# Attentions of successive images side by side, with banks of their own, in a network of four layers

## The reference: what is computed

```
# layer 0: attention with 32 channels           x = Wp @ softmax(q k / sqrt(32)) v + x
# layer 1: bottleneck with a deformable 3x3 convolution
off = conv3x3(h); y, x = grid + off             # per pixel and tap: where to sample
samp = bilinear(h, y, x) * sigmoid(mask)        # 9 taps x 4 corners, gathered
x = relu(bn(w3 @ relu(bn(w2 @ samp))) + x)
# layer 2: attention with 16 query channels     x = gamma * (softmax(q k) v) + x
# layer 3: group norm, then attention with 128 channels
h = group_norm(x); w = softmax(q(h) k(h) / sqrt(128))
x = (x + Wp @ (w v(h))) / sqrt(2)
```

## Time and profile before

| | |
|---|---|
| device time, median of 3 runs | 571.77 us (570.62 to 573.72) |
| profiled execution, its own time | 573.63 us |
| its span, first to last instruction | 571.6 us |
| busy: PE, DVE, ACT, POOL | 491.7, 316.8, 288.4, 293.3 us |
| mean granted TensorE clock | 0.91 of full |

### The profile page before, as it was taken

One profiled execution on the slowest core, in us unless ns is written; L12 is line 12 of the kernel. 1 busy time (PEld: TensorE's weight loads), 2 busy tenths in 40 slices (PEclk: granted clock), 3 DMA queues, 4 the chain that ended last, 5 costly groups with the idle time before them and its releaser, 6 DMA issues.

```text
span 571.6 us, 7362 instructions
## 1 busy us (share of the span) xinstructions
PE 491.7 (86%) x2688; PEld 328.6 (57%) x2688; DVE 316.8 (55%) x558; ACT 288.4 (50%) x485; POOL 293.3 (51%) x292
## 2 busy tenths in 40 slices
PE   5897897869889778889998969998957999896996
PEld 3443633525435346856686845776844677693775
DVE  4746225476556766766678556558565525624321
ACT  4275461374177655245575434584532557442652
POOL 0000177777777777777777777777777300000000
PEclk9999778659879879979999979999987899997999
DMA  5000111112212111211313111112111100100000
GB/s 218 0 1 1 46 56 50 56 47 58 86 46 94 46 52 48 55 47 46 94 47 92 52 46 52 50 54 87 52 52 46 28 1 1 38 1 0 1 1 37
DMA packets 12562, 26.92 MB, mean 47 GB/s; under 512 B 4976, under 2 KB 5616, under 8 KB 12528
## 3 DMA queue, kind: packets, MB, share of 16 engines
q0 software_dynamic: 9216, 18.89, 11.7%
q1 hardware_dynamic: 2880, 6.52, 3.0%
q10 hardware_dynamic: 432, 1.05, 0.5%
HBM read 21.99 MB, written 4.46 MB: 46 GB/s over the span
## 4 chain that ended last, share of the span: by engine, by line
POOL 49%; PE 26%; issue 15%; DVE 3%; ACT 3%; DMA 2%; POOLq 0%; DVEq 0%; ACTq 0%
POOL got L298 49%; PE pd L604 5%; PE pq L596 2%; PE pc L586 2%; PE pa L586 2%; PE pq L363 2%; PE pa L334 2%; DMA xall<-x_dram 1%; PE pa L541 1%; PE pc L541 1%; DVE neg_max L1601 1%; PE pc L388 1%; PE pc L334 1%; PE pa L570 1%; PE pd L328 1%
## 5 line engine op out<-in xcount | busy, mean ns | idle before, releaser
L298 POOL DMA_INDIRECT got<-cell_table,rows_all x288 | 293.1, 1018 | 155.4 <-issue 87.5
L1601 DVE TENSOR_REDUCE neg_max<-pa 128x1 f32<-128x1024 f32 x48 | 58.7, 1223 | 39.7 <-PE pa L334 39.3
L604 PEld LDWEIGHTS pd<-v3T,probsT 128*128 128x128 f32 x512 | 60.3, 192 | 11.1 <-ACT probsT L1112 8.5
L604 PE MATMUL pd<-v3T,probsT 128*128 128x128 f32 x512 | 63.3, 277 | 3.2 <-ACT probsT L1112 2.4
L363 PE MATMUL pq<-q_stack,k_stack 128*128 128x512 f32 x120 | 55.1, 516 | 9.5 <-ACT expT L1141 5.1
L334 PE MATMUL pa<-k_stack,q_stack 96*128 96x512 f32 x96 | 40.2, 505 | 10.5 <-DVE neg_max L1601 7.3
L1141 ACT ACTIVATE expT<-pq 128x512 f32<-128x512 f32 x64 | 35.6, 595 | 23.9 <-PE pq L363 23.0
L363 PEld LDWEIGHTS pq<-q_stack,k_stack 128*128 128x128 f32 x120 | 24.6, 217 | 36.2 <-ACT expT L1141 11.9
L1678 DVE TENSOR_TENSOR weighed<-got,corner_w 128x1152 f32<-128x1152 f32 x32 | 43.3, 1354 | 3.2 <-DMA got<-cell_table,rows_all 2.1
L1112 ACT ACTIVATE probsT<-pq 128x1024 f32<-128x1024 f32 x32 | 32.7, 1022 | 15.0 <-PE pq L596 10.3
L1225 ACT ACTIVATE expT<-pq 128x512 f32<-128x512 f32 x56 | 31.1, 598 | 15.4 <-PE pq L363 14.3
(11 more groups left out here) (173 smaller groups left out, 788.6 us busy)
## 6 DMA issues: line engine op xcount, KB each, us to landing
got<-cell_table,rows_all POOLq DMA_INDIRECT x288, 2.5
cell_table<-tabS SPq DMA_DIRECT2D x4, 512.0 KB, 2.6
out_dram<-cells SPq DMA_DIRECT2D x8, 256.0 KB, 2.1
xall<-x_dram SPq DMA_DIRECT2D x2, 512.0 KB, 8.6
wts<-weights_dram SPq DMA_DIRECT2D x1, 778.5 KB, 6.1
xall<-x_dram ACTq DMA_DIRECT2D x2, 256.0 KB, 5.2
xall<-x_dram ACTq DMA_DIRECT2D x1, 512.0 KB, 8.4
cell_table<-tabS SPq DMA_DIRECT2D x4, 64.0 KB, 2.7
```

The source lines that it names most:

```text
L298: nc.gpsimd.indirect_dma_start(got[:, t, k, :], None, tables[b % 2], bass.IndirectOffsetOnAxis(ap=rows_all[:, b, at:at + 1], axis=0)).then ...
L604: last = nc.tensor.matmul(d0[:, 0:C], probsT[:, tile(j)], v3T[:, j, :], start=j == 0, stop=j == TILES - 1)
L1601: nc.vector.tensor_reduce(neg_max[:, t:t + 1], pair[:, :], axis=X, op=ALU.max, negate=True)\
```

## The change

1. Banks. For images 1 and 2, layer 3 has pa for its scores, b0 for turned probabilities, v and end, and d0 for values. Layer 2 has pc for qk, scores and (as c0, c1) values, and b1 for v and shifted scores. Layer 2 of the last image alternates shifted scores between b1 and d1. Layer 3 of the last image, which has no partner, alternates between pairs again, and its turned halves between b0 and b1.
2. Halves. l3_turn(b, t) becomes l3_turn(b, t, g): 4 transposes and one ACT copy of 512 columns for each half g. l2_v and l3_v work by halves in one bank.
3. Order. All lists of calls are new. l3(b) and l2(b + 1) are woven together from their first tiles to their last, for b = 0, 1, 2. Layer 3 of image b therefore starts when layer 1 of image b + 1 is about to end. The lists of layers 0 and 1 are new as well, and the very first calls too: l0_v(0) stands ahead of l0_qk(0, 0).

Number and shape of the matmuls stay as they are; there are 32 more ACT copies for the turned halves (64 of 512 columns for 32 of 1024), and 4 more for l2_v.

```diff
-
-        def e2_bank(h, j):
-            return (b0, b1)[j % 2] if h == 0 else (b0, b1, a0)[j % 3]
-
-        def e_free(h, j):
-
+
+
+        LAST = BATCH - 1
+
+        def w3_banks(b):
+            return pc if b else pa
+
+        def v2_bank(b, h):
+            return b1 if b else (c0, c1)[h]
+
+        def s2_pair(b):
+            return pc if b else pa
+
+        def shift2_bank(b, h):
+            if b == 0:
+                return (b1, c1)[h]
+            return c1 if b == LAST and h else d1
+
+        def e2_bank(b, h, j):
+            if b == 0:
+                return (b0, b1)[j % 2] if h == 0 else (b0, b1, a0)[j % 3]
+            return (b1, d1)[j % 2] if b == LAST else b1
+
+        def e_free(b, h, j):
+
+            if b:
+                return max(TILES * h + j - (b == LAST), 0)
             return {(0, 0): 0, (0, 1): 0, (1, 0): TILES - 1, (1, 1): TILES, (1, 2): 0}.get(
                 (h, j), TILES * h + j + 1 - (2, 3)[h])
 
-        def o2_bank(t):
-            return (a1, c0, d0)[t % 3][:, 0:C + 1]
+        def o2_bank(b, t):
+            return ((c0, c1)[t % 2] if b else (a1, c0, d0)[t % 3])[:, 0:C + 1]
+
+        def tr2_bank(b, h):
+            return (b1, c0)[h] if b else (c1, b0)[h]
+
+        def k3_banks(b):
+            return pc if b == LAST else pa
+
+        def v3_bank(b, h):
+            return (b0, b1)[h] if b == LAST else b0
+
+        def s3_pair(b, t):
+            return (pa, pc)[t % 2] if b == LAST else pa
+
+        def pt_bank(b, g):
+            return (b0, b1)[g] if b == LAST else b0
+
+        def o3_bank(b, t):
+            return ((d0, d1)[t % 2] if b == LAST else d0)[:, 0:C]
+
+        def tr3_bank(b, h):
+            return (b0, b1)[h] if b == LAST else b0
 
         @block.sync
         def _(sp):
...
                 if b == 0:
                     pe.wait_ge(shift0_done, 2 * BATCH)
                 else:
-                    pe.wait_ge(exp3_done, TILES * b - 1)
+                    pe.wait_ge(mom_ready, b)
                 for c in (0, 2, 1, 3):
                     if c == 1:
                         pe.wait_ge(w3_mm, 4 * b + 2)
-                    nc.tensor.matmul(pa[:, c * N // 4:(c + 1) * N // 4], wt("w3")[quarter(c), :], h2[quarter(c), :],
+                    nc.tensor.matmul(w3_banks(b)[:, c * N // 4:(c + 1) * N // 4], wt("w3")[quarter(c), :], h2[quarter(c), :],
...
-                if b == 0 and t:
-                    pe.wait_ge(max2_done, t)
-                if b and t == 1:
-                    pe.wait_ge(v2_ready, b + 1)
-                if b and t >= 2:
-                    pe.wait_ge(max2_done, TILES * b + t - 1)
-                scores(t, 0, s2_pair(b, t), s2_mm)
+                else:
+                    pe.wait_ge(max2_done, TILES * b + t)
+                scores(t, 0, s2_pair(b), s2_mm)
 
...
             def l2_shifted(b, h, j):
                 if j == 0:
                     pe.wait_ge(shift2_done, 2 * b + h + 1)
-                if e_free(h, j):
-                    pe.wait_ge(exp2_done, 2 * TILES * b + e_free(h, j))
-                shifted_scores(h, j, 0, e2_bank(h, j), t2_mm)
+                    pe.wait_ge(v2_ready, 2 * b + 2)
+                if e_free(b, h, j):
+                    pe.wait_ge(exp2_done, 2 * TILES * b + e_free(b, h, j))
+                shifted_scores(h, j, 0, e2_bank(b, h, j), t2_mm)
...
             def l3_k(b, h):
                 pe.wait_ge(h3_ready, 2 * b + h + 1)
-                nc.tensor.matmul(pc[:, half(h)], wt("wk3"), h3[:, half(h)], start=True, stop=True).then_inc(k3_mm, 1)
+                if b and b < LAST:
+                    pe.wait_ge(exp3_done, TILES * b)
+                nc.tensor.matmul(k3_banks(b)[:, half(h)], wt("wk3"), h3[:, half(h)], start=True, stop=True).then_inc(k3_mm, 1)
 
             def l3_q(b, h):
                 pe.wait_ge(h3_ready, 2 * b + h + 1)
+                if b < LAST:
+                    pe.wait_ge(k3_ready, 2 * b + h + 1)
+                else:
+                    pe.wait_ge(exp3_done, TILES * b)
                 nc.tensor.matmul(pa[:, half(h)], wt("wq3"), h3[:, half(h)], start=True, stop=True).then_inc(q3_mm, 1)
...
             def l3_scores(b, t):
                 if t == 0:
                     pe.wait_ge(q3_ready, 2 * b + 2)
                     pe.wait_ge(k3_ready, 2 * b + 2)
-                if t >= 2:
+                elif b < LAST:
+                    pe.wait_ge(exp3_done, TILES * b + t)
+                elif t >= 2:
                     pe.wait_ge(exp3_done, TILES * b + t - 1)
-                pair = (pa, pc)[t % 2]
                 for h in range(2):
-                    last = nc.tensor.matmul(pair[:, half(h)], q3[:, tile(t)], k3[:, half(h)], start=True, stop=True)
+                    last = nc.tensor.matmul(s3_pair(b, t)[:, half(h)], q3[:, tile(t)], k3[:, half(h)], start=True, stop=True)
                 last.then_inc(s3_mm, 1)
 
-            def l3_turn(b, t):
+            def l3_turn(b, t, g):
+
                 pe.wait_ge(exp3_done, TILES * b + t + 1)
+                copies = 2 * (TILES * b + t) + g - (b == LAST)
                 if t == 0:
                     pe.wait_ge(v3_ready, 2 * b + 2)
-                else:
-                    pe.wait_ge(pt_copied, TILES * b + t)
+                if t or (g and b < LAST):
+                    pe.wait_ge(pt_copied, copies)
+                for j in range(4):
+                    last = nc.tensor.transpose(pt_bank(b, g)[:, tile(j)], probs[:, t % 2, tile(4 * g + j)], ident)
+                last.then_inc(pt_mm, 1)
+
+            def l3_values(b, t):
+                pe.wait_ge(pt_copied, 2 * (TILES * b + t) + 2)
+                if b < LAST and t:
+                    pe.wait_ge(o3_norm, TILES * b + t)
+                elif b == LAST:
+                    if t >= 2:
+                        pe.wait_ge(o3_norm, TILES * b + t - 1)
+                    elif t:
+                        pe.wait_ge(exp2_done, 2 * TILES * BATCH)
                 for j in range(TILES):
-                    last = nc.tensor.transpose(pq[:, tile(j)], probs[:, t % 2, tile(j)], ident)
-                last.then_inc(pt_mm, 1)
-
-            def l3_values(b, t):
-                pe.wait_ge(pt_copied, TILES * b + t + 1)
-                if t:
-                    pe.wait_ge(o3_norm, TILES * b + t)
-                for j in range(TILES):
-                    last = nc.tensor.matmul(d0[:, 0:C], probsT[:, tile(j)], v3T[:, j, :], start=j == 0, stop=j == TILES - 1)
+                    last = nc.tensor.matmul(o3_bank(b, t), probsT[:, tile(j)], v3T[:, j, :], start=j == 0, stop=j == TILES - 1)
                 last.then_inc(o3_mm, 1)
...
-            def l3_turn(b, t):
-                act.wait_ge(pt_mm, TILES * b + t + 1)
-                if t:
+            def l3_turn(b, t, g):
+                act.wait_ge(pt_mm, 2 * (TILES * b + t) + g + 1)
+                if t and g == 0:
                     act.wait_ge(o3_mm, TILES * b + t)
-                copy(probsT[:, :], pq[:, :]).then_inc(pt_copied, 1)
+                copy(probsT[:, half(g)], pt_bank(b, g)).then_inc(pt_copied, 1)
...
```

More of the change, by code:

```diff
@@ L766, in _ @@
             l0_out(2, 3)
             l0_turn(2, 3)
-            for n in range(6):
+            l1_conv1(2, 0)
+            l0_scores(3, 5)
+            l0_scores(3, 6)
+            l1_conv1(2, 1)
+            l0_scores(3, 7)
+            l0_shift(3, 0)
+            l0_shift(3, 1)
+            l0_shifted(3, 0, 0)
+            l0_shifted(3, 0, 1)
+            l1_table(2, 0)
+            l1_turn(0, 5)
+            for n in range(2, 5):
                 l0_shifted(3, 0, n)
-            l1_turn(0, 3)
@@ L853, in _ @@
[L853 to L855 removed]
+            l1_turn(1, 4)
+            l1_turn(1, 5)
             l3_k(0, 0)
@@ new lines, in _ @@
+            l2_scores(2, 4)
+            l3_turn(1, 2, 0)
+            l2_shifted(2, 0, 0)
+            l3_scores(1, 4)
+            l2_shifted(2, 0, 1)
+            l3_turn(1, 2, 1)
+            l2_scores(2, 5)
+            l2_shifted(2, 0, 2)
+            l2_shifted(2, 0, 3)
+            l2_scores(2, 6)
+            l3_values(1, 2)
+            l3_turn(1, 3, 0)
+            l3_scores(1, 5)
+            l3_turn(1, 3, 1)
+            l2_shifted(2, 0, 4)
+            l2_scores(2, 7)
+            l1_turn(3, 1)
@@ new lines, in _ @@
+            for n in range(5, 8):
+                l2_shifted(2, 0, n)
+            l2_shift(2, 1)
+            l3_values(1, 3)
+            l3_turn(1, 4, 0)
+            l2_shifted(2, 1, 0)
+            l2_values(2, 0)
+            l3_turn(1, 4, 1)
+            l2_shifted(2, 1, 1)
+            l2_shifted(2, 1, 2)
+            l2_values(2, 1)
+            l1_turn(3, 2)
+            l2_shifted(2, 1, 3)
+            l3_values(1, 4)
+            l2_shifted(2, 1, 4)
+            l3_scores(1, 6)
+            l2_shifted(2, 1, 5)
@@ L972, in _ @@
+            l3_turn(1, 7, 0)
+            l2_turn(2, 1)
+            l3_turn(1, 7, 1)
+            l1_turn(3, 5)
+            l3_end(1, 0)
+            l3_groups(2)
```

(11 more changed lines are left out.)

1524 lines of the change are left out of this document (814 added, 710 removed).

## The result

| | median us | of runs | profiled run, its span, clock |
|---|---|---|---|
| before | 572.05 | 570.62 to 573.72 (4) | 573.63, 571.6, 0.910 |
| changed | 580.28 | 579.42 to 580.91 (4) | 579.42, 577.4, 0.905 |

The ratio is 1.0137 with a 95% interval of 1.0106 to 1.0168, so the changed kernel is 8 us slower. The profiled execution is its fastest; the spans of the other three are 577.9 to 578.9. Ratios in this text leave out two executions that ran far above the others of their kernel (one of old_front at 1019 us, one of the new order at five taps at 579.7).

What follows compares the result with a forecast made beforehand. Time was taken as the last gather's landing plus PE's remaining work: 450.0 + 2.9 + 71.2 + 6.4 + 46.5 = 577.0 us of span, 5.4 above 571.6, so a median of 577.2 us, range 569.5 to 584.5.

Steps and rivals of the forecast that it cites:

- Last landing at 450.0: End of GpSimd's gathers: first gather 1 us earlier at 67.4, train length kept, last data landing at 450.
- the head's loss: Image 0's start: l0_v(0) ahead of l0_qk(0) makes the cells 1.5 to 2 us later.
- The turn of the last tile at 452.9, 2.9 us behind it: Tile (3, 7): weighing, adding and PE's turn take 2.9 us after landing, so the turn comes at 452.9.
- 14.8 us more behind the turn, less 3.2: PE from l1_turn(3, 7) to l2_turn(3, 1): 14.8 us of l3(2) added, 3.2 taken off, 59.6 becoming 71.2.
- Gain and loss of the weaving: Behind the last turn: filling waits with a second attention and having one pair each were taken to cancel.
- The stalls of "about 5 us": PE from the last turn to l2_turn(3, 1): stalls of about 5 of 59.6 us, left as they were.
- Group norm 6.4: Last image's group norm: 5.7 us plus DVE's l3_end(2, 0) at 0.65, giving 6.4.
- last layer 46.5: Last fourth layer: 50.8 us less 2.8 for q and k at full clock and 1.5 for halves, 46.5.
- Everything ahead costs nothing: All work ahead of image 2's group norm is covered by the gathers, 95.2 us per image, PE needing 86.0.
- Interlocking pairs: Rival: single banks in images 1 and 2 expose waits between engines, 583 to 588 us; chance 0.15 for 581 to 588.
- Weaving pays: Rival: 5 us of stalls behind the turn vanish and the start wins 3, 570 us; chance 0.14 shared with no effect.
- No effect: Rival: PE's whole work sets the time, so order doesn't matter, 571 to 574 us; chance 0.14 shared with weaving.

Runs made afterwards that it cites:

- old_front: Changed kernel with the call lists of the kernel before on PE, ACT and DVE up to image 0's group norm: 579.41 us, ratio 1.0132.
- five taps: 5 of 9 gathers per tile of images 1 to 3: kernel before 566.16 us, changed kernel 571.67, changed kernel with the earlier lists up to image 0's group norm 563.02.
- new front: Changed kernel's call lists up to image 0's group norm; put into the kernel before, all else its own: 587.02 us, ratio 1.0264.
- new rest: Changed kernel's calls behind image 0's group norm; with the kernel before's lists ahead of them ratio 1.0132, with its own 1.0137.
- late_weigh: Changed kernel with weighing and adding of tiles (3, 5) and (3, 6) moved behind l3_norm(2) on DVE, their turns and copies likewise: 583.06 us, ratio 1.0240.
- early_weigh: Kernel before with only l1_weigh and l1_add of (3, 4) and l1_weigh of (3, 5) put between l2_values(2, 1) and (2, 2) on DVE: 583.46 us, ratio 1.0227.
- eight taps: 8 instead of 9 gathers for each tile of image 3: kernel before 567.87 us (ratio 0.9927), changed kernel 573.75 us (1.0019).
- late_weigh_l3: late_weigh, and part of image 2's fourth attention (scores, v, half turns, values) moved ahead of l1_turn(3, 7): 597.26 us, ratio 1.0458.
- old_front_late: late_weigh_l3 with the call lists of the kernel before up to image 0's group norm: 593.61 us, ratio 1.0413.
- new_last: Kernel before with only the last fourth attention as in the changed kernel (call order, halves, values in two banks): 570.79 us, ratio 0.9985.
- old rest: Kernel before's calls behind image 0's group norm; with the changed kernel's lists ahead of them 587.02 us, ratio 1.0264.

## Why the prediction was right

It said 577.2 us for 580.28, and 577.0 for the span of 577.4. The mechanism held: the last tile is turned at nearly the same time as before, and PE has 7.6 us more behind it. One path to that turn I had not seen, and that it meets the one I named is luck.

**Last landing at 450.0.** It was near 450.4, for partly wrong reasons. I had the first gather at 67.4; it was at 69.1, since the rows come at 68.6, 3.6 later than before. The train was 0.8 shorter than I had it (378.8 for 379.6), which gave half of the 1.7 us back. In the other profiles with the new front the rows came at 69.5 to 70.3, with the old one at 64.2 to 66.0. I had put the head's loss at 1.5 to 2 us. Both halves of q and k now wait behind the 16 matmuls of l0_v(0) (the first half ran at 4.97 and is now at 10.93, the first scores at 17.43 for 15.66), which makes 1.8 us. The other 1.9 come further down the list; which calls make them was not tried.

**The turn of the last tile at 452.9, 2.9 us behind it.** It was 453.8. I said that PE would wait and that DVE would be at (3, 6) or (3, 7) when it did. It was at (3, 5): as DVE goes in order, the group norm of image 2 comes 20 us behind that tile's landing, and the turn 7.6 us behind the group norm. These 7.6 us are the same in all five profiles with the new rest as it is, also in the three with fewer gathers, where DVE never waits for data. So in the changed kernel the turn hangs on tile (3, 5) over the group norm, and the last landing, which I had named, comes 0.5 us ahead of its weighing. That both paths end so close is luck, but it also makes the sum robust: in late_weigh, which frees the group norm of tile (3, 5), DVE waits for the last landing (1.9 us), the turn is 2.8 us behind that weighing's start, and nothing is won. (With the gathers of the changed kernel that turn would be at some 453.3, an estimate from 450.4 and 2.8.) So the wait at (3, 5) is not what costs in the changed kernel, and what is left is the l3(2) work behind the turn, which the prediction took from the lists. early_weigh shows what the placing does where that work stands ahead of the turn: with an unchanged list on PE it costs 13 us (10.3 of it at the turn in the profile).

**14.8 us more behind the turn, less 3.2.** 11.6 was forecast. The stretch that the sum has, from the turn to the end of l2_turn(3, 1), took 69.8 us for 71.2 and was 59.6 before. PE is busy in it for 67.5 us where it was for 57.3, so 10.2 longer, and idle for 2.3 us both times. Gain and loss of the weaving cancel, as I had let them; the moved work was 1.4 us less than my prices made it. The stalls of "about 5 us" in the prediction were these 2.3. From turn to end it took 123.5 to 123.7 us in four kernels with the new rest (125.2 in the fifth, at eight taps, with the clock at 0.98 for 1.00), and 115.7 to 116.3 in the five with the old one unchanged behind the turn. No run shortened this tail: that less work behind the turn would win the time back is argued from the sum, and the two attempts, late_weigh_l3 and old_front_late, brought other waits in.

**Group norm 6.4, last layer 46.5.** The first was 6.2 (523.6 to 529.8), the second 47.6. q and k ran at the full clock as forecast, 1.88 us for four in place of 3.78, and values(7) started 3.22 us behind values(6) for the 3.2 forecast. The halves, though, are little of what shortens it: new_last has the same 3.22 us, and its stretch behind the group norm is 0.4 us shorter where the changed kernel's is 2.1. I read the rest as that of the group norm with work in it, since the clock there is 1.00 for 0.93; no run has that part alone.

**Everything ahead costs nothing.** True of this kernel, and only by the cover that I named. The new front costs 15 us in the old rest and 9 at five taps. In the changed kernel it lies under the wait for image 3's tiles: with the old front back the turn is 0.8 us earlier (453.0).

**The rivals.** Interlocking pairs did not set the time: from the turn to l2_turn(3, 1) PE is idle for 2.3 us, as before, and what they cost ahead of it is covered, since old_front waits 16.1 us for data there. But the mechanism is real: in late_weigh_l3 the l2_scores(3, n) that have only one another wait 1.3 us each on their one pair. "Weaving pays" is true by some 3 us where the gathers don't bind, at the edge of what can be measured. "No effect" fell. What I had not weighed is a slow front in the new list, because I looked at the stages only for whether they fit under the gathers.

The forecast change was 5.4 us; the medians differ by 8.2 and the profiled spans by 5.8. The difference lies in which executions were profiled: that of the kernel before is 1.6 us above its median, that of the changed kernel is its fastest, 0.9 below. So the spans match the sum better than the change does. The head alone moved by up to 1.8 us between the profiled executions of kernels with this front. Which calls of the new front cost how much was not tried.

## What to carry to other kernels

With an engine that goes in order, the place of a wait counts more than its length: look for what stands behind it in the same list and leads to work on another engine. The sum to make for a change of order is the time behind a landing that can't move, and a gain ahead of that landing was worth nothing here while the work behind it stayed. But work moved ahead of a wait must have something beside it, and nothing that waits for it may stand ahead of the landed tile: alone it took 1.7 times its length, DVE reached the tile 17 us after it had landed, and its partner was left alone too.

## What the runs showed of the hardware

TensorE's mean granted clock was lower in stretches in which PE had more gaps. In the stretch of layer 2 alone in late_weigh_l3 it was busy for 27.2 of 35.8 us and the clock was 0.68; woven, in the changed kernel, it was busy for 68.6 of 72.0 at 1.00. In the kernel before, from 69 to 165 us, it was busy for 79.3 of 96.0 us at 0.77. The busy share alone doesn't tell the clock: the changed kernel has 78.5 of 96.0 us at 0.73 from 69 to 165 us, and 78.3 of 96.0 at 0.89 from 165 to 261. A pair of 96x512 matmuls took 1.22 us with layer 2 alone and 0.73 woven (two levels, 1.2 and 2.4 GHz). So a removed filler is paid twice, in idle time and in slower matmuls around it: up to the last group norm, late_weigh_l3 had 4 us less PE busy time behind its turn than the changed kernel (64.6 us for 68.6) and took 2.4 us more; old_front_late has the same two numbers. The Trainium skill (TensorE: Matmul & The Clock Gate, Part 1) has the throttled level as the one that activity releases; these stretches agree.
